# Attention units of two head kinds: score banks from both row halves of TensorE, value products cut at the head change

## The reference, cut to what matters

```
idx = clip(pos[None, :] - pos[:, None], -20, 20) + 20
attn1 = einsum('bhqd,bhkd->bhqk', q, k)
attn2 = einsum('bhqd,qkd->bhqk', q, rel_k[idx])
attn = softmax((attn1 + attn2) / sqrt(8))
w1 = einsum('bhqk,bhkd->bhqd', attn, v)
w2 = einsum('bhqk,qkd->bhqd', attn, rel_v[idx])
x = (w1 + w2)  ->  x @ Wo.T + bo
```

## Time and profile before

| what | value |
|---|---|
| median of 3 runs | 2585.8 us (2581.75 to 2586.46) |
| the profiled execution, its own time | 2584.21 us |
| its span, first to last instruction | 2582.4 us |
| TensorE busy | 2293.3 us, 89% |
| VectorE busy | 1905.0 us, 74% |
| ScalarE busy | 1584.7 us, 61% |
| GpSimd busy | 1038.4 us, 40% |
| mean granted TensorE clock | 0.950 |

### The profile page before, as it was taken

One profiled execution on the slowest core, in us unless ns is written; L12 is line 12 of the kernel. 1 busy time (PEld: TensorE's weight loads), 2 busy tenths in 40 slices (PEclk: granted clock), 3 DMA queues, 4 the chain that ended last, 5 costly groups with the idle time before them and its releaser, 6 DMA issues. The chain is left out here.

```text
span 2582.4 us, 102624 instructions
## 1 busy us (share of the span) xinstructions
PE 2293.3 (89%) x37544; PEld 1609.2 (62%) x37544; DVE 1905.0 (74%) x3734; ACT 1584.7 (61%) x3954; POOL 1038.4 (40%) x1350
## 2 busy tenths in 40 slices
PE   5773599999999999999998999869999996999999
PEld 3441477767767677677676777646666664666665
DVE  5663488878878788788787888637676764777777
ACT  3442477778777777777777777637777772232322
POOL 5664445545554555455445554300000002333332
PEclk9886799999999999999999999959999997999999
DMA  6887345544544455455444554300010101101010
GB/s 191 271 271 205 87 108 120 115 108 110 122 107 111 102 124 112 106 116 123 104 115 105 121 112 105 67 25 26 24 37 24 37 25 58 37 24 37 24 37 16
DMA packets 568188, 243.42 MB, mean 94 GB/s; under 512 B 462278, under 2 KB 531526, under 8 KB 563142
## 3 DMA queue, kind: packets, MB, share of 16 engines
q1 hardware_dynamic: 567750, 237.52, 36.7%
HBM read 134.13 MB, written 103.29 MB: 92 GB/s over the span
## 5 line engine op out<-in xcount | busy, mean ns | idle before, releaser
L886 ACT ACTIVATE a_probs<-a_bank_s,a_neg_max 128x512 f32<-128x512 f32 x1024 | 694.6, 684 | 184.2 <-DVE a_neg_max L821 180.1
L821 DVE TENSOR_REDUCE a_neg_max<-a_bank_s 128x2 f32<-128x1024 f32 x512 | 627.0, 1225 | 56.0 <-ACT a_probs L886 3.7
L673 PE MATMUL a_bank_pt<-a_ident,a_probs 128*128 128x128 f32 x4096 | 573.1, 283 | 8.5 <-issue 2.6
L673 PEld LDWEIGHTS a_bank_pt<-a_ident,a_probs 128*128 128x128 f32 x4096 | 445.1, 143 | 116.4 <-issue 79.1
L866 ACT ACTIVATE a_probs_t<-a_bank_pt 128x512 f32<-128x512 f32 x512 | 305.9, 597 | 201.4 <-PE a_bank_pt L673 196.0
L807 DVE COPY a_probs_t<-a_bank_pt 128x512 f32<-128x512 f32 x512 | 350.1, 684 | 32.4 <-PE a_bank_pt L673 24.5
L662 PE MATMUL a_bank_s<-a_k,a_q 48*32 48x512 bf16 (+15 forms) x4096 | 274.1, 290 | 94.0 <-DMA a_kl<-scr_parts 65.0
L699 PE MATMUL a_bank_o<-a_probs_t,a_v 128*32 128x32 f32 (+2 forms) x15872 | 305.8, 228 | 2.0 <-issue 2.0
L699 PEld LDWEIGHTS a_bank_o<-a_probs_t,a_v 128*32 128x32 f32 x15872 | 245.8, 112 | 58.8 <-ACT a_probs_t L866 48.4
L662 PE MATMUL a_bank_s<-a_kl,a_q 48*32 48x204 bf16 (+14 forms) x3840 | 241.4, 266 | 23.6 <-ACT a_probs L886 19.1
L800 DVE TENSOR_TENSOR a_bank_s<-a_bank_s,a_win 128x144 f32<-128x144 f32 (+2 forms) x640 | 164.2, 275 | 125.9 <-PE a_bank_s L662 113.1
(11 more groups left out here) (161 smaller groups left out, 3600.1 us busy)
## 6 DMA issues: line engine op xcount, KB each, us to landing
scr_probs<-a_probs SPq DMA_DIRECT2D x256, 144.0 KB, 5.2
a_raw<-scr_qr SPq DMA_DIRECT2D x256, 96.0 KB
scr_qr<-p_qr SPq DMA_DIRECT2D x64, 320.0 KB, 2.9
a_feat<-scr_probs SPq DMA_DIRECT2D x256, 78.0 KB
scr_parts<-p_sp SPq DMA_DIRECT2D x144, 128.0 KB, 2.9
a_left<-scr_probs SPq DMA_DIRECT2D x256, 64.0 KB, 2.5
a_q<-scr_parts SPq DMA_DIRECT2D x32, 192.0 KB
a_k<-scr_parts SPq DMA_DIRECT2D x32, 192.0 KB
```

The source lines that it names most:

```text
L673: ins = nc.tensor.transpose(b_pt[bank_of(job)][:, 0, t * P:(t + 1) * P], probs[(u - 1) % 4][:, j, MAX_REL + t * P:MAX_REL + (t + 1) * P], ...
L821: nc.vector.tensor_reduce(neg_max[:, 2 * pair:2 * pair + 2], b_s[:, 2 * pair:2 * pair + 2, :], AX.X, ALU.max, negate=True).then_inc(max_ok, 1)
L886: nc.scalar.activation(probs[u % 4][:, j, MAX_REL:MAX_REL + S], b_s[:, j, :], ACT.Exp, bias=neg_max[:, j:j + 1], accum_out=sums[:, t, j, u ...
```

## The change

A unit keeps its tile of queries but mixes two kinds of heads. Query blocks 0 and 1 hold the heads of kind u % 4, query blocks 2 and 3 those of kind (u % 4) xor 1, which have the other parity and so lie in the other row half. The banks are permuted: bank p holds query block PLACES[p], so banks 0 and 1 hold the blocks 0 and 2, and banks 2 and 3 the blocks 1 and 3. The two banks of a pair now come from different row halves. The program order stays: all matmuls of one bank, then all of the other.

In `attended` a piece may no longer reach over the border between block 1 and block 2, since the heads change there: 128 becomes 64 + 64, 96 becomes 32 + 64. The matmuls are 80 a unit for t = 0 and 88 for t > 0. The write of scr_probs becomes two DMAs of half the size, each for two blocks, and the thresholds of p_out double. The window add and the sums only get other addresses.

```
+PLACES = (0, 2, 1, 3)
+def head_of(u, i):
+    return u % 4 ^ i // 2
...
-                    sp.wait_ge(p_out[k], b * 16 * NT + 16 * (u // 4))
+                    sp.wait_ge(p_out[k], b * 32 * NT + 32 * (u // 4))
...
-                    at = PROBS_AT[t % 2] + u % 4 * NJ * QBLK * WIN
-                    own = probs[u % 4][:, 0, t * P:]
-                    sp.dma_start(bass.AP(scr["probs"].tensor, at, [[WIN, P], [H * QBLK * WIN, NQB], [1, WIN]]),
...
+                    for i in (0, 2):
+                        at = PROBS_AT[t % 2] + (i * H + head_of(u, i) * NJ) * QBLK * WIN
+                        own = probs[u % 4][:, PLACES.index(i), t * P + i * QBLK:]
+                        sp.dma_start(bass.AP(scr["probs"].tensor, at, [[WIN, P], [H * QBLK * WIN, 2], [1, WIN]]),
+                                     bass.AP(own.tensor, own.offset,
+                                             [own.ap[0], [2 * (S + 2 * MAX_REL) + QBLK, 2], [1, WIN]])
+                                     ).then_inc(p_out[u % 4], 16)
...
-                par = slice((u % 2) * HALF, (u % 2) * HALF + ROWS)
-                for i in pair:
+                for p in pair:
+                    i = PLACES[p]
                     at = u // 4 * P + i * QBLK
                     edge = max(at - MAX_REL, 0)
                     for keys, a, z in ((KL, 0, edge), (K, edge, S)):
                         if a == z:
                             continue
+                        par = head_of(u, i) % 2 * HALF
                         for g in range(NJ):
-                            half = (NJ * g + u % 4) // 2
-                            ins = nc.tensor.matmul(b_s[g * QBLK:(g + 1) * QBLK, i, a:z], Q[s][par, half, at:at + QBLK],
-                                                   keys[s][par, half, a:z], start=a == 0, stop=z == S,
+                            half = (NJ * g + head_of(u, i)) // 2
+                            ins = nc.tensor.matmul(b_s[g * QBLK:(g + 1) * QBLK, p, a:z],
+                                                   Q[s][par:par + ROWS, half, at:at + QBLK],
+                                                   keys[s][par:par + ROWS, half, a:z], start=a == 0, stop=z == S,
...
-                        parts = [(n * QBLK, (n + 1) * QBLK, EDGES.index(max(n * QBLK - MAX_REL, 0)))
-                                 for n in range(NQB)]
+                        parts = [(n, n + 1, EDGES.index(max(n * QBLK - MAX_REL, 0))) for n in range(NQB)]
                     elif kt == t - 1:
-                        parts = [(0, QBLK, EDGES.index(P - MAX_REL)), (QBLK, P, EDGES.index(P))]
+                        parts = [(0, 1, EDGES.index(P - MAX_REL)), (1, 2, EDGES.index(P)), (2, 4, EDGES.index(P))]
                     else:
-                        parts = [(0, P, EDGES.index(P if kt < t else 0))]
+                        parts = [(n, n + 2, EDGES.index(P if kt < t else 0)) for n in (0, 2)]
...
+                                                   probs_t[u % 2][:, p:p + 2 * (hi - lo) - 1:2,
...
-                        need(act, p_out[u % 4], b, 16 * NT, 16 * t)
+                        need(act, p_out[u % 4], b, 32 * NT, 32 * t)
```

More of the change, by code:

```diff
@@ L623, in row @@
                     sp.wait_ge(exp_ok, b * 4 * UNITS + 4 * u + 4)
-                    at = PROBS_AT[t % 2] + u % 4 * NJ * QBLK * WIN
-                    own = probs[u % 4][:, 0, t * P:]
-                    sp.dma_start(bass.AP(scr["probs"].tensor, at, [[WIN, P], [H * QBLK * WIN, NQB], [1, WIN]]),
-                                 bass.AP(own.tensor, own.offset, [own.ap[0], [S + 2 * MAX_REL + QBLK, NQB], [1, WIN]])
-                                 ).then_inc(p_out[u % 4], 16)
+                    for i in (0, 2):
[5 more added lines that the diff above has]
+                                     ).then_inc(p_out[u % 4], 16)
             for sm, start in ((y_st, 16), (y_ok, 2)):
@@ L678, in attended @@
             def attended(b, u, s):
-                t, hh = u // 4, u % 4
+                t = u // 4
                 after = (b, u + 1) if u < UNITS - 1 else (b + 1, 0)
@@ L686, in attended @@
                     need(pe, o_ev, b, 1, 0)
-                first = hh == 0
+                first = u % 4 == 0
                 for kt in range(NT):
                     if kt == t:
-                        parts = [(n * QBLK, (n + 1) * QBLK, EDGES.index(max(n * QBLK - MAX_REL, 0)))
-                                 for n in range(NQB)]
+                        parts = [(n, n + 1, EDGES.index(max(n * QBLK - MAX_REL, 0))) for n in range(NQB)]
                     elif kt == t - 1:
-                        parts = [(0, QBLK, EDGES.index(P - MAX_REL)), (QBLK, P, EDGES.index(P))]
+                        parts = [(0, 1, EDGES.index(P - MAX_REL)), (1, 2, EDGES.index(P)), (2, 4, EDGES.index(P))]
                     else:
-                        parts = [(0, P, EDGES.index(P if kt < t else 0))]
+                        parts = [(n, n + 2, EDGES.index(P if kt < t else 0)) for n in (0, 2)]
                     for lo, hi, edge in parts:
+                        p, hh = PLACES.index(lo), head_of(u, lo)
                         for j in range(NJ):
-                            out = b_o[32 * j:32 * j + 32, 0, t * P + lo:t * P + hi].rearrange("p (i q) -> p i q", q=QBLK)
-                            ins = nc.tensor.matmul(out, V[s][:, V_SLOTS.index((edge, kt)), j, hh * 24:hh * 24 + 32],
-                                                   probs_t[u % 2][:, lo // QBLK:hi // QBLK,
+                            out = b_o[32 * j:32 * j + 32, 0, t * P + lo * QBLK:t * P + hi * QBLK]
+                            ins = nc.tensor.matmul(out.rearrange("p (i q) -> p i q", q=QBLK),
+                                                   V[s][:, V_SLOTS.index((edge, kt)), j, hh * 24:hh * 24 + 32],
+                                                   probs_t[u % 2][:, p:p + 2 * (hi - lo) - 1:2,
                                                                   kt * P + j * QBLK:kt * P + (j + 1) * QBLK],
@@ L791, in add_window @@
             def add_window(u, pair):
-                t, hh = u // 4, u % 4
+                t = u // 4
                 first, last = t == 0 and pair == 0, t == NT - 1 and pair == 1
-                for i, n in ((0, 1), (1, 1)) if first or last else ((0, 2),):
-                    i += 2 * pair
+                for k, n in ((0, 1), (1, 1)) if first or last else ((0, 2),):
+                    p = 2 * pair + k
+                    i = PLACES[p]
                     edge = t * P + i * QBLK - MAX_REL
                     a, z = max(edge, 0), min(edge + WIN, S)
-                    whole = b_s[:, i, a:z]
-                    near = bass.AP(whole.tensor, whole.offset, [whole.ap[0], [S + QBLK, n], [1, z - a]])
-                    ins = nc.vector.tensor_tensor(near, near, win[t % 2][:, i:i + n, hh, a - edge:z - edge], ALU.add)
+                    whole, own = b_s[:, p, a:z], win[t % 2][:, i, head_of(u, i), a - edge:z - edge]
+                    near = bass.AP(whole.tensor, whole.offset, [whole.ap[0], [S + 2 * QBLK, n], [1, z - a]])
+                    step = (2 * NJ + head_of(u, 2) - head_of(u, 0)) * WIN
+                    ins = nc.vector.tensor_tensor(near, near, bass.AP(own.tensor, own.offset, [own.ap[0], [step, n], [1, z - a]]),
+                                                  ALU.add)
                 return ins
@@ L886, in row @@
                             nc.scalar.activation(probs[u % 4][:, j, MAX_REL:MAX_REL + S], b_s[:, j, :], ACT.Exp,
-                                                 bias=neg_max[:, j:j + 1], accum_out=sums[:, t, j, u % 4:u % 4 + 1]
+                                                 bias=neg_max[:, j:j + 1], accum_out=sums[:, t, PLACES[j], head_of(u, PLACES[j]):head_of(u, PLACES[j]) + 1]
                                                  ).then_inc(exp_ok, 1)
```

## The result

The changed kernel takes 2726.2 us (median of 4 runs, 2717.1 to 2737.2) against 2584.4 for the kernel before beside it: a ratio of 1.055, interval 1.051 to 1.059. It is 142 us slower where 2564 was predicted. The profiled execution of the changed kernel took 2737.2 us with a span of 2735.4.

What follows compares the result with a forecast made beforehand. VectorE paces most of a tile, TensorE the stretch around `features`. Ordinary tiles 21.1 us, row starts -5.9, jumps 2.8, VectorE's small waits 3: 21 us off 2584.2, 2563.2; runs' median 1.6 higher, so 2564, range 2547 to 2584.

Steps and rivals of the forecast that it cites:

- The scores: Score matmuls on TensorE: two banks on different row halves stream together, a pair takes 0.35 us for 0.55, gain 0.20.
- In order: Rival, score pairs: second bank starts only after the first one's KL columns; 0.14 us a pair, 2574 us; chance 0.18.
- halves one at a time: Rival, score pairs: row halves don't stream together, a pair stays at 0.55 us; 8.5 us slower, 2594; chance 0.09.
- mix pair: Evidence from the program mix: two score products in different row groups take 1.06 us, taken to show that they run together.
- The sum without the cuts: The forecast's sum over the program: 21 us gained, 2564 us; it counted the cuts at only 0.06 us a tile.
- key waits at row starts: TensorE's wait for the last key load at about 8 row starts: grows from 0.68 to about 1.6 us.
- The value products: Cuts in `attended`: eight matmuls more cost 0.02 us, three such cuts in every unit 0.06; bounds 0.03 and 0.1.
- On the path or not: In a tile only two of eight score pairs and one of four `attended` lie where TensorE sets the end.
- The fixed cost of a matmul: Rival, cuts in `attended`: about 60 cycles per matmul, 0.6 us for 24 more; 2598 us or so; chance 1 in 100.

Runs made afterwards that it cites:

- e7: The kernel before with every value product cut to single blocks of 32 queries: 3098.6 us, 1.198 of the kernel before.
- e1: The kernel before with only the extra cuts of the value products, heads and rows unchanged: 2753.7 us, 1.066 of the kernel before.
- e2: The changed kernel with the value products uncut, part of the results wrong: 2562.6 us, 0.991 of the kernel before.
- e3: The changed kernel with all scores from key table K, 3,840 fewer matmuls, cuts kept: 2575.5 us, 0.9966 of the kernel before.
- e8: The change applied to the kernel before in units 2 and 3 of each tile only: 2686.4 us, 1.0402 of the kernel before.

## Why the prediction was wrong

**The scores** were right. A pair takes 0.36 us for the 0.35 forecast, and both banks' KL matmuls stand in one group of eight. "In order" and "halves one at a time" are both out. In the pair at 1107.27 the second bank's KL matmuls start at 1107.30, before the first bank's K matmuls at 1107.40. Had they followed the first bank's 268 KL columns, the pair would have taken 0.12 us longer (0.23 x 268 / 512, an estimate). The Trainium skill, "TensorE: Matmul & The Clock Gate", Part 3, has matmuls strictly first in, first out in start and end. This trace, like the mix pair, doesn't agree with it.

**The sum without the cuts** was right. It was 21 us and 2564; the kernel with uncut products has 22 us and 2562.6. One of its parts was too low: the key waits at row starts grew to 19.0 us in 7 waits in the window, from 2.7 in 6. That is 2.7 us each, for about 1.6 forecast. For the whole to come out as it did, others must have given a little more than I took; which, I did not separate, so the close sum is in part luck.

**The value products** are the step that failed: "So a cut of eight matmuls more costs 0.02 us. The change makes three such cuts in every unit: 0.06. Only one `attended` of four is on the path." The time in the array was right, 1.12 us for 88 matmuls. The step took that time for the whole cost. It was read from 64 matmuls against 56, in one unit, in which TensorE did not stop. The wait for the next block of instructions, which no term of the sum has, was put at nothing without a reason. Over the program the cuts add 12,288 instructions, and each such pair of matmul and load costs 27 to 30 ns on the average of the two kernels with all units cut (this one and e7): 164 us and not 4. "On the path or not" did not apply, since a late block stops whatever unit it falls in: the changed kernel has such stops in all four units of a tile.

What supports this cause: the cuts alone give the loss (1.066), the rest without them the forecast gain (0.991); the same cuts with 3,840 fewer score matmuls cost nothing (0.997); those score matmuls alone are worth only 0.4% (0.996), and every stop ends 1.1 to 2.0 us after a block's packet, in the changed kernel whole blocks after the last stop. The traffic, my first suspicion for the late blocks, is out as the main cause.

**The fixed cost of a matmul**, given 1 in 100, was the only rival in the right direction for the right operation. Its mechanism is not what the trace shows, since 88 matmuls still take 1.12 us when their instructions are there. But its sum, some 0.6 us for 24 more matmuls, 25 ns each, is close to the measured 27 ns, by luck. By the Trainium skill, "TensorEngine Tiling (Array Packing)", Instruction Overhead, about 60 cycles go with each matmul. The timeline doesn't agree inside a block, and the total only happens to. I had weighed the figure of the Trainium skill against one unit's array time alone.

**What was in view.** The profile before had it: the queue for instructions on the page (282 packets), TensorE's 3.65 us for issue behind each jump, and 4,508 matmuls in 200 us. I read the last as a load on the array and never as a load on its supply of instructions.

**The clock** goes with it. TensorE's granted clock was 0.98 in the stage before, 0.95 after, 0.93 in e1 and 0.86 in e7. Behind the stop that ended at 1091.86, eight transposes take 1.09 us at a granted clock of 1.00 and soon after 1.97 at 0.50, which is the lower of its two levels, 1.2 GHz:

```profile
1092.12 1.09 PE L685 MATMUL a_bank_pt<-a_ident,a_probs 128*128 128x128 f32 x8
...
1093.66 1.97 PE L685 MATMUL a_bank_pt<-a_ident,a_probs 128*128 128x128 f32 x8
```

From e2 to the changed kernel TensorE's busy time grew from 2221.9 to 2289.1 us, from the kernel before to e1 from 2293.3 to 2373.9. The cuts' own time in the array, 0.02 us for each of three in 256 units, makes some 15 of that (an estimate). And e1 waits less for issue than the changed kernel (110 us for 157 in the window), though it takes 27 us longer. How much of the loss is the clock and how much the stops was not separated.

**What stays open.** No run shows what makes a packet start as late as it does, so late that TensorE is through with its instructions. It is not the other DMA traffic, beyond some 27 us of it, nor the packets' own length. That the score matmuls were worth more (39 ns) than the cuts cost (27), and that the same number of cuts costs 68, 73 or 102 us by their place, is not derived from it either. No version here that computes the whole attention beats the kernel before; how to keep the 0.991 with right results was not tried.

## What to carry to other kernels

Before splitting an operation, count the instructions that it adds on that engine per us, beside the time in the array. In this kernel TensorE was supplied with at most some 50 instructions a us (matmuls and weight loads, 25 pairs) over a long window; it ran at 45, and 20% more matmuls cost 5.5%. The average alone does not decide: e3 ran at 48 without a loss, e8 at 45.5 with one of 4%. The sign to look for is idle gaps "for issue" in the middle of an unrolled group, whole blocks of instructions apart, each ending soon after a packet of the instruction queue. Where there are next to none, as in the kernel before, removing instructions gave almost nothing.

## What the runs showed of the hardware

- In all twelve kernels instruction blocks of 16 KB reached the core at most 248 times in 1200 us, with the DMA engines 51% busy or 9%. A block's packet took about 1.1 us, and in the changed kernel at least 3.5 us lay between the starts of two in a straight run.
- TensorE's stops within a straight run of the changed kernel come at block ends, a whole number of blocks of 121 to 124 matmuls with their weight loads after the last stop (98 of 98). They last up to 2.8 us there and 3.1 in e7, even between the sixth and the seventh of eight equal transposes, and in all twelve kernels end 1.1 to 2.0 us after a packet of the instruction queue (752 of 752).
- Matmuls on the two row halves of TensorE, each with four column groups, stream together: 16 pieces over 512 columns and two banks in 0.36 us, where two banks on one half take 0.55.
